# Attention and fp8 feed-forward on one core: variance from ScalarE's squares, up weights scaled in their turning product, first aggregation on GpSimd, x rounded in PSUM by TensorE, in a new order

## The chip, the cores and the metric

The kernel runs on one core of a Trainium2 chip. The metric is the device time of one execution in microseconds (us); lower is better. A time given for a kernel is the median of its runs.

## What is computed

x is 4 batches of 256 rows by 256 channels, ctx is 4 x 256 x 128. The reference, cut to what matters:

```python
# attention: energy from ctx alone, x enters normalised
query, key = ctx @ Wq.T + bq, ctx @ Wk.T + bk
attention = softmax(query @ key.T)
x = x + layernorm(x) @ attention.T
# feed-forward on layernorm(x), all three products with fp8-rounded operands
qx, sx, sc = quantize(layernorm(x))            # row scale = max|row| / 448
g = qlinear(qx, sx, sc, w_gate)                # 704 x 256 each, weight rows
u = qlinear(qx, sx, sc, w_up)                  # scaled by max|row| / 448 and rounded
t = silu(g) * u                                # 1024 x 704
qt, st, sct = quantize(t)
x = x + qlinear(qt, st, sct, w_down)           # 256 x 704
```

The rounding to fp8 is done by adding and subtracting a "grid": a number per element, a power of two times a large constant with some bits more, so that fp32's own rounding cuts the value to fp8's mantissa. `grid_w`, `grid_x`, `grid_d` and `grid_t` are these for the up and gate weights, x, the down weights and t.

## The kernel before

It is written engine by engine: every engine has a list of calls, written out by hand, that it works off in order, and semaphores join the lists. P is 128, b counts the four batches, i the eight tiles of 128 rows (two to a batch), k the six chunks of 128 gate and up rows, h halves.

**Attention.** TensorE projects q and k (`project_q`, `project_k`, one per half), forms the scores (`scores`), VectorE takes their negated maximum (`score_max`), ScalarE the exponentials (`exps`), VectorE puts 1/z on the diagonal of a 128x128 matrix (`spread_of_z`), and TensorE turns and scales the attention in one fp32 product with it (`transpose_att`, L1143). `attend` (L1154) multiplies by the rows of x, and VectorE's `residual` (L758) makes x1 out of the result, 1/std of the first normalisation and x.

**Weights.** For chunk k: VectorE takes peaks, reciprocals and scales (`peak_of_up`, `reciprocal_up`, `scales_up`), ScalarE multiplies (`scale_up`), VectorE makes the grid (`exponents_up`, `floor_up`), GpSimd adds and subtracts it (`add_grid_up`, `subtract_up`), ScalarE multiplies by the row's peak (`dequantise`, L566), TensorE turns the chunk (`transpose_up`, L1178), ScalarE copies it out of bank_a as `w_hi` (`evac_up`) and VectorE keeps the rest of the fp32 value as `w_lo` (`split_up`, L875). There is one bank for this, so `transpose_up(k)` waits for `split_up(k - 1)`, and the first `gates` waits for all six.

**x.** First statistics are of x (`bn_stats1`, `bn_aggr1`, then GpSimd's `add_eps1`, `rstd1_of`), second ones of x1 (`bn_stats2`, `bn_aggr2`). ScalarE centres x1 (`centre_x1`), VectorE takes the peak and makes the grid and the sum (`peak_of_x`, `grids_x`, `add_grid_x` L813), GpSimd subtracts (`subtract_x`, L396), TensorE turns the bf16 result (`transpose_qx`, L1166), ScalarE copies it out (`evac_qxT`).

**Feed-forward.** For each tile i, `gates(i)` and `ups(i)` (L1197) are eight matmuls each, 352 columns wide, into gate_ps and up_ps. ScalarE's `silu`, VectorE's `hidden` (t, L885), `peak_of_t`, `grids_t`, `add_grid_t`, GpSimd's `subtract_t`, TensorE's `transpose_t`, ScalarE's `evac_tT`, TensorE's `down`, VectorE's `scale_y` and a last addition follow. gate_ps and up_ps have one buffer each, so `gates(i)` waits for `silu(i - 1)` and `ups(i)` for `hidden(i - 1)`. The last tile goes in two halves.

**Down weights.** They are rounded like the others, turned by two DMA transposes on SyncE's queue, scattered to their order in device memory by six indirect DMAs that GpSimd issues (`scatter(k)`, L357), and read back; `down(0)` waits for that.

`keep_warm`, `keep_clock` (L1276) and `keep_busy` are matmuls on zeros whose results nobody reads.

## Time and profile before

| | |
|---|---|
| median of 3 runs | 80.45 us (80.34 to 80.68) |
| the profiled execution's own time | 80.45 us |
| its span, first to last instruction | 78.6 us |
| outside the span | 1.85 us |
| TensorE busy | 69.5 us, 88% |
| VectorE busy | 69.1 us, 88% |
| ScalarE busy | 52.0 us, 66% |
| GpSimd busy | 54.1 us, 69% |
| granted TensorE clock, mean of the span | 1.000 |

In the profile's rows PE is TensorE's matmuls, PEld its weight loads, DVE VectorE, ACT ScalarE, POOL GpSimd and SP SyncE; a q behind a name is that engine's sequencer. An fp32 matmul stands in two records, a transpose and a bf16 matmul in one. The ends of matmuls are modelled and overlap the next start, so that the cost of a group of them is read from its start to the start of what follows without a wait.

### The profile page before, as it was taken

To read this page: it belongs to the slowest core of one execution; us is meant where nothing else is said; L and a number is where in the kernel's file an instruction comes from. 1 tells how busy PE (TensorE), PEld (TensorE's weight loads), DVE (VectorE), ACT (ScalarE), POOL (GpSimd) and SP (SyncE) were. 2 spreads that over 40 slices of the span, in tenths; PEclk is the share of its full clock that TensorE was granted. 3 is DMA by queue.
4 is the path that set the end of the run, shared out by engine and by line. 5 is a ranking of instruction groups with operands and counts; after the bars stand their busy time and mean duration, and the time that the engine had idled before them with its cause. 6 is when DMAs were issued, how large, how long until landed. Compare 5 with 4: busy or idle time off the path is not lost.

```text
span 78.6 us, 1481 instructions
## 1 busy us (share of the span) xinstructions
PE 69.5 (88%) x449; PEld 57.7 (73%) x449; DVE 69.1 (88%) x180; ACT 52.0 (66%) x102; POOL 54.1 (69%) x66
## 2 busy tenths in 40 slices
PE   4999998999749599294999999999799999985996
PEld 4945837988549489272998999979698699744575
DVE  1019999999899999999999999999999999999860
ACT  0615799999966999897877472937924557446400
POOL 5000008973999999985687989899954667985960
DMA  0899999900000000004140201110033001030143
GB/s 18 289 389 388 330 360 397 379 20 0 0 4 4 0 0 8 0 0 91 32 77 0 75 0 33 33 38 0 17 88 112 4 22 53 0 133 0 41 159 133
DMA packets 6839, 7.33 MB, mean 93 GB/s; under 512 B 2256, under 2 KB 5200, under 8 KB 6832
## 3 DMA queue, kind: packets, MB, share of 16 engines
q1 hardware_dynamic: 6064, 5.97, 23.1%
q10 hardware_dynamic: 576, 0.92, 3.3%
q0 software_dynamic: 192, 0.36, 1.5%
q8 instruction: 3, 0.05, 0.3%
q14 instruction: 4, 0.03, 0.1%
HBM read 5.44 MB, written 1.41 MB: 87 GB/s over the span
## 4 chain that ended last, share of the span: by engine, by line
DVE 30%; POOL 25%; PE 22%; issue 15%; DMA 6%; SPq 1%; POOLq 0%; DVEq 0%
POOL q_w L407 6%; DVE t_sb L885 6%; DMA x_sb<-x_dram 6%; PE gate_ps L1197 5%; PE up_ps L1197 5%; DVE peak_w L820 4%; POOL rstd L371 3%; PE gate_ps L1269 3%; POOL sum_w L403 3%; POOL x_sb L435 3%; POOL yscale L417 2%; DVE grid_w L772 2%; PE bank_c L1154 2%; POOL q_t L424 2%; DVE peak_d L850 2%
## 5 line engine op out<-in xcount | busy, mean ns | idle before, releaser
L403 POOL TENSOR_TENSOR sum_w<-sum_w,grid_w 128x512 f32<-128x512 f32 x5 | 5.7, 1155 | 11.9 <-DVE grid_w L777 11.9
L424 POOL TENSOR_TENSOR q_t<-sum_t,grid_t 128x704 bf16<-128x704 f32 x7 | 10.9, 1554 | 3.9 <-DVE sum_t L915 3.9
L1197 PE MATMUL gate_ps<-w_hi,qxT 128*128 128x352 f32 x32 | 10.7, 337 | 1.2 <-issue 1.2
L1197 PE MATMUL up_ps<-w_hi,qxT 128*128 128x352 f32 x32 | 10.8, 340 | 0.4 <-DVE t_sb L885 0.4
L590 ACT ACTIVATE act_g<-gate_ps,rowscale 128x704 f32<-128x704 f32 x8 | 6.7, 843 | 5.3 <-PE gate_ps L1197 5.3
L1197 PE MATMUL gate_ps<-w_lo,qxT 128*128 128x352 f32 x32 | 10.3, 323 | 0.0
L1197 PE MATMUL up_ps<-w_lo,qxT 128*128 128x352 f32 x32 | 10.3, 323 | 0.0
L604 ACT ACTIVATE tT<-bank_b 128x768 bf16<-128x768 bf16 x7 | 5.7, 809 | 5.6 <-PE bank_c L1241 3.2
L1154 PE MATMUL bank_c<-attT,xT 128*128 128x256 f32 x32 | 7.7, 383 | 1.5 <-DVE x L758 1.5
L357 POOL DMA_INDIRECT wdnT_order<-wdnT,idx_sb x6 | 7.0, 1164 | 1.6 <-issue 1.6
L597 ACT ACTIVATE abs_t<-t_sb 128x704 bf16<-128x704 f32 x8 | 6.3, 786 | 2.4 <-DVE t_sb L885 2.4
L1154 PEld LDWEIGHTS bank_c<-attT,xT 128*128 128x128 f32 x32 | 5.8, 190 | 2.4 <-issue 1.7
L1197 PEld LDWEIGHTS gate_ps<-w_hi,qxT 128*128 128x128 f32 x32 | 6.0, 188 | 1.7 <-issue 1.4
L885 DVE TENSOR_TENSOR t_sb<-up_ps,act_g 128x704 f32<-128x704 f32 x8 | 7.1, 887 | 0.1
L915 DVE SCALAR_TENSOR_TENSOR sum_t<-t_sb,s_t,grid_t 128x704 f32<-128x704 f32 x7 | 6.9, 984 | 0.3
L890 DVE TENSOR_REDUCE peak_t<-t_sb 128x1 f32<-128x704 f32 x8 | 7.0, 881 | 0.0
L713 DVE BATCH_NORM_STATS2 bn<-x_sb 128x6 f32<-128x256 f32 x8 | 3.0, 413 | 4.5 <-DMA x_sb<-x_dram 4.5
L407 POOL TENSOR_TENSOR q_w<-sum_w,grid_w 128x512 bf16<-128x512 f32 x6 | 6.8, 1161 | 0.2
L1197 PEld LDWEIGHTS up_ps<-w_hi,qxT 128*128 128x128 f32 x32 | 6.0, 188 | 0.8 <-ACT qxT L547 0.7
L1197 PEld LDWEIGHTS up_ps<-w_lo,qxT 128*128 128x128 f32 x32 | 6.0, 188 | 0.0
L1197 PEld LDWEIGHTS gate_ps<-w_lo,qxT 128*128 128x128 f32 x32 | 6.0, 188 | 0.0
L566 ACT ACTIVATE sum_w<-q_w,peak_w 128x256 f32<-128x256 bf16 x12 | 5.2, 507 | 1.1 <-POOL q_w L407 1.1
(105 smaller groups left out, 190.8 us busy)
## 6 DMA issues: line engine op xcount, KB each, us to landing
x_sb<-x_dram SPq DMA_DIRECT2D x4, 256.0 KB, 8.7
xT<-x_t_dram SPq DMA_DIRECT2D x2, 512.0 KB, 8.9
out_dram<-x_sb SPq DMA_DIRECT2D x8, 128.0 KB, 1.7
wup_sb<-w_gate_up_dram ACTq DMA_DIRECT2D x3, 256.0 KB, 5.7
wup_sb<-w_gate_up_dram SPq DMA_DIRECT2D x3, 256.0 KB, 5.9
wdn_sb<-w_down_dram SPq DMA_DIRECT2D x1, 704.0 KB, 9.3
ctx_sb<-ctx_t_dram SPq DMA_DIRECT2D x2, 256.0 KB, 4.8
wdnT_in_order<-wdnT_order SPq DMA_DIRECT2D x1, 320.0 KB, 2.8
```

The costliest lines, as they stand in the source:

```text
L357: nc.gpsimd.indirect_dma_start(out=wdnT_order, out_offset=bass.IndirectOffsetOnAxis(ap=idx_sb[0:fresh[k], k:k + 1], axis=0), in_=wdnT[0:fr ...
L403: nc.gpsimd.tensor_tensor(sum_w[:, k], sum_w[:, k], grid_w[:, k], ALU.add).then_inc(sum_w_done[k], 1)
L407: nc.gpsimd.tensor_tensor(q_w[:, k], sum_w[:, k], grid_w[:, k], ALU.subtract).then_inc(q_w_done, 1)
L424: nc.gpsimd.tensor_tensor(q_t[:, i % 2], sum_t[:, i % 2], grid_t[:, i % 2], ALU.subtract)\
L590: nc.scalar.activation(halves(act_g[:, i % 3]), gate_ps[:, :, 0:IH], ACT.Silu, scale=rowscale[:, i:i + 1]).then_inc(silu_done, 1)
L597: nc.scalar.activation(abs_t[:, i % 2], t_sb[:, i % 2], ACT.Abs, scale=GRID)\
L604: nc.scalar.activation(tT[:, i % 2], tT_ps, ACT.Copy).then_inc(tT_evac, 1)
L885: nc.vector.tensor_tensor(halves(t_sb[:, i % 2]), up_ps[:, :, 0:IH], halves(act_g[:, i % 3]), ALU.mult).then_inc(t_done, 1)
L890: nc.vector.tensor_reduce(peak_t[:, i:i + 1], t_sb[:, i % 2], AX_X, ALU.max, apply_absolute_value=True).then_inc(peak_t_done, 1)
L915: nc.vector.scalar_tensor_tensor(sum_t[:, j], t_sb[:, j], s_t[:, col], grid_t[:, j], ALU.mult, ALU.add)\
L1154: last = nc.tensor.matmul(xm_ps[:, j], xT[:, b, c, j * P:(j + 1) * P], attT[:, b, c], start=(c == 0), stop=(c == NC - 1))
L1197: last = nc.tensor.matmul(ps[:, h, 0:IH], qxT[:, b, c, j * P:(j + 1) * P].bitcast(F32R), w[:, c, a, h * IH:(h + 1) * IH].bitcast(F32R), st ...
```

## The change

Five things are changed.

- The second statistics go from VectorE to others: `residual` gives the row sum as well (`accum_out`), ScalarE centres with it (everything is N times as large from there on), and ScalarE squares the centred rows and sums them (`squares_x`). `bn_stats2` and `bn_aggr2` are gone.
- `bn_aggr1` is gone; GpSimd joins the two halves of the first statistics in five small operations.
- `dequantise` is gone: the peaks stand on the diagonal of `spread_w`, made by GpSimd, and `transpose_up` is an fp32 product with it.
- `add_grid_x`, `subtract_x` and `transpose_qx` are gone: TensorE adds x times a diagonal of scales, plus the grid, minus the grid, in PSUM (`quantise_x`). GpSimd makes the diagonals (`spread_of_sx`).
- `spread_of_z` is one instruction where it was two, `yscale_of` serves two tiles at once, and all five lists and the order of the loads are new.

```diff
             def centre_x1(b):
-                act.wait_ge(stats2_done, b + 1)
+                act.wait_ge(x1_done, b + 1)
...
-                                                bias=mv2[:, i, 0:1], scale=-1.0)
+                                                bias=total2[:, i:i + 1], scale=-float(N))
                 last.then_inc(xc2_done, 1)
+            def squares_x(b):
+                act.wait_ge(xc2_done, b + 1)
+                for j in range(LT):
+                    i = LT * b + j
+                    last = nc.scalar.activation(wup_sb[:, b, j], xc2[:, b, j], ACT.Square, accum_out=var2[:, i:i + 1])
+                last.then_inc(stats2_done, 1)
...
+            def spread_of_w(k):
+                after("ident")
+                pool.wait_ge(peak_w_done, k + 1)
+                for a in range(2):
+                    last = nc.gpsimd.tensor_scalar(spread_w[:, k, a], ident[:, :], peak_w[:, k, a:a + 1], 1.0, ALU.mult,
+                                                   ALU.mult)
+                last.then_inc(spread_w_done, 1)
...
+            def spread_of_sx(b):
+                pool.wait_ge(s_x_done, b + 1)
+                after("ident")
+                for j in range(LT):
+                    i = LT * b + j
+                    last = nc.gpsimd.tensor_scalar(spread_sx[:, b, j], ident[:, :], s_x[:, i:i + 1], 1.0, ALU.mult,
+                                                   ALU.mult)
+                last.then_inc(spread_sx_done, 1)
...
                     last = nc.vector.scalar_tensor_tensor(x1[:, b, j], xm_ps[:, j], rstd1[:, i:i + 1],
-                                                          x_sb[:, b, j], ALU.mult, ALU.add)
+                                                          x_sb[:, b, j], ALU.mult, ALU.add,
+                                                          accum_out=total2[:, i:i + 1])
...
-            def transpose_qx(b):
-                pe.wait_ge(q_x_done, b + 1)
+            def quantise_x(b):
+                pe.wait_ge(xc2_done, b + 1)
+                pe.wait_ge(spread_sx_done, b + 1)
+                pe.wait_ge(grid_x_done, b + 1)
...
+                blocks = [(c, j) for c in range(NC) for j in range(LT)]
+                for c, j in blocks:
+                    nc.tensor.matmul(qxT_ps[:, c, j * P:(j + 1) * P], xc2[:, b, j, c * P:(c + 1) * P],
+                                     spread_sx[:, b, j], start=((c, j) == blocks[0]), stop=False)
+                for c, j in blocks:
+                    nc.tensor.matmul(qxT_ps[:, c, j * P:(j + 1) * P], grid_x[:, b, j, c * P:(c + 1) * P],
+                                     identb[:, :], start=False, stop=False)
+                for c, j in blocks:
+                    last = nc.tensor.matmul(qxT_ps[:, c, j * P:(j + 1) * P], grid_x[:, b, j, c * P:(c + 1) * P],
+                                            minus_identb[:, :], start=False, stop=((c, j) == blocks[-1]))
                 last.then_inc(qxT_ready, 1)
...
             def transpose_up(k):
-                pe.wait_ge(deq_done, k + 1)
+                pe.wait_ge(q_w_done, k + 1)
+                pe.wait_ge(spread_w_done, k + 1)
...
-                        last = nc.tensor.transpose(wuT_ps[:, c, a], deq_w[:, k, a, c * P:(c + 1) * P], ident[:, :])
+                        last = nc.tensor.matmul(wuT_ps[:, c, a], q_w[:, k, a, c * P:(c + 1) * P], spread_w[:, k, a],
+                                                start=True, stop=True)
```

On SyncE's queue the loads were ctx 0, x 0, up 1, up 3, ctx 1, xT 0, up 5, x 1, down, x 2, x 3, xT 1, and are now ctx 1, ctx 0, up 1, up 3, x 0, xT 0, down, x 2, x 3, up 5, x 1, xT 1.

TensorE's list from the second chunk of weights to just before the first `gates`, before; bank_a with ident is `transpose_up`, bank_c is `attend`, up_ps with spread_rz `transpose_att`, bank_b with warm_w `keep_clock` and bank_d `transpose_qx`:

```order
L1178 MATMUL bank_a<-ident,sum_w 128x128 x4
L1143 MATMUL up_ps<-spread_rz,att 128x128 x4
L1178 MATMUL bank_a<-ident,sum_w 128x128 x4
L1154 MATMUL bank_c<-attT,xT 128x256 x4
L1276 MATMUL bank_b<-warm_w 128x128 x4
L1178 MATMUL bank_a<-ident,sum_w 128x128 x4
L1143 MATMUL up_ps<-spread_rz,att 128x128 x4
L1178 MATMUL bank_a<-ident,sum_w 128x128 x4
L1166 MATMUL bank_d<-identb,q_x 128x128 x4
L1154 MATMUL bank_c<-attT,xT 128x256 x4
L1178 MATMUL bank_a<-ident,sum_w 128x128 x4
```

and the same stretch of TensorE's list now, where bank_a with spread_w is `transpose_up` and the three rows of bank_d are `quantise_x`:

```order
L1198 MATMUL bank_a<-spread_w,sum_w 128x128 x4
L1297 MATMUL bank_b<-warm_w 128x128 x6
L1154 MATMUL up_ps<-spread_rz,att 128x128 x4
L1198 MATMUL bank_a<-spread_w,sum_w 128x128 x4
L1165 MATMUL bank_c<-attT,xT 128x256 x4
L1198 MATMUL bank_a<-spread_w,sum_w 128x128 x4
L1297 MATMUL bank_b<-warm_w 128x128 x2
L1179 MATMUL bank_d<-spread_sx,xT 128x128 x4
L1182 MATMUL bank_d<-identb,grid_x 128x128 x4
L1185 MATMUL bank_d<-minus_identb,grid_x 128x128 x4
L1198 MATMUL bank_a<-spread_w,sum_w 128x128 x4
L1165 MATMUL bank_c<-attT,xT 128x256 x4
```

A rounding of x is twelve matmuls in place of four, a transpose of weights is a product, and four `keep_clock` calls of two matmuls stand in this stretch where two stood. Up to the first `gates` there are 20 matmuls of `keep_clock` now and 12 before; behind it none now and 8 before.

GpSimd's list around the scatters, before; q_x is `subtract_x`, q_t is `subtract_t`, the DMA rows are `scatter`:

```order
L396 TENSOR_TENSOR q_x<-sum_x,grid_x 128x512
L357 DMA wdnT_order<-wdnT,idx_sb 704x256 x2
L390 TENSOR_TENSOR rowscale<-rstd,peak_x 128x2
L396 TENSOR_TENSOR q_x<-sum_x,grid_x 128x512
L357 DMA wdnT_order<-wdnT,idx_sb 704x256
L424 TENSOR_TENSOR q_t<-sum_t,grid_t 128x704
L357 DMA wdnT_order<-wdnT,idx_sb 704x256 x2
L390 TENSOR_TENSOR rowscale<-rstd,peak_x 128x2
L396 TENSOR_TENSOR q_x<-sum_x,grid_x 128x512
L424 TENSOR_TENSOR q_t<-sum_t,grid_t 128x704
```

and now:

```order
L450 TENSOR_SCALAR spread_sx<-ident,s_x 128x128 x4
L358 DMA wdnT_order<-wdnT,idx_sb 704x256
L405 TENSOR_SCALAR ve<-var 128x4
L358 DMA wdnT_order<-wdnT,idx_sb 704x256 x4
L466 TENSOR_TENSOR q_t<-sum_t,grid_t 128x704
L411 TENSOR_TENSOR rstd<-ve,minus_half 128x4
L417 TENSOR_TENSOR rowscale<-rstd,peak_x 128x2 x2
L450 TENSOR_SCALAR spread_sx<-ident,s_x 128x128 x2
L466 TENSOR_TENSOR q_t<-sum_t,grid_t 128x704
```

Five scatters now stand ahead of the first `subtract_t`, and the second half's 1/std, row scales and the last `spread_of_sx` stand behind that. Further down the list, `subtract_t(4)` stands ahead of `subtract_t(3)`.

## Rows read from the trace of the kernel before

**Rows 1.** Page, part 1: busy time, share, instructions.

```profile
PE 69.5 (88%) x449; PEld 57.7 (73%) x449; DVE 69.1 (88%) x180; ACT 52.0 (66%) x102; POOL 54.1 (69%) x66
```

**Rows 2.** Page, part 4: the chain that ended last, by engine.

```profile
DVE 30%; POOL 25%; PE 22%; issue 15%; DMA 6%; SPq 1%; POOLq 0%; DVEq 0%
```

**Rows 3.** Busy time by stretch (start:end, length, engines, clock, DMA share, GB/s).

```profile
1.10:20.60 19.50, 19.13 (x90) 14.50 (x90) 14.90 (x41) 14.65 (x37) 7.37 (x10) 1.00 0.73 259
20.60:37.53 16.93, 11.74 (x77) 10.05 (x76) 16.57 (x55) 14.46 (x33) 15.14 (x15) 1.00 0.07 14
37.53:65.64 28.11, 27.56 (x192) 25.18 (x193) 27.65 (x65) 18.07 (x28) 21.90 (x25) 1.00 0.15 40
```

**Rows 4.** Timeline of TensorE, first 17 us (start, us, what, idle before).

```profile
1.11 2.93 PE L1281 MATMUL gate_ps<-warm_w 128*128 128x128 f32 x12 [1.11 <-DVE warm_w L956]
...
13.37 1.13 PE L1143 MATMUL up_ps<-spread_rz,att 128*128 128x128 f32 x8 [0.16 <-DVE spread_rz L749]
14.34 1.06 PE L1276 MATMUL bank_b<-warm_w 128*128 128x128 f32 x8
```

**Rows 5.** Timeline of TensorE, 24 to 38 us.

```profile
24.49 0.60 PE L1178 MATMUL bank_a<-ident,sum_w 128*128 128x128 f32 x4
24.93 1.06 PE L1143 MATMUL up_ps<-spread_rz,att 128*128 128x128 f32 x8
26.88 0.63 PE L1178 MATMUL bank_a<-ident,sum_w 128*128 128x128 f32 x4 [0.89 <-DVE w_lo L875]
...
29.07 1.05 PE L1276 MATMUL bank_b<-warm_w 128*128 128x128 f32 x8
29.96 0.62 PE L1178 MATMUL bank_a<-ident,sum_w 128*128 128x128 f32 x4
...
32.91 0.63 PE L1178 MATMUL bank_a<-ident,sum_w 128*128 128x128 f32 x4 [1.44 <-DVE w_lo L875]
33.68 0.40 PE L1166 MATMUL bank_d<-identb,q_x 128*128 128x128 bf16 x4
33.92 1.95 PE L1154 MATMUL bank_c<-attT,xT 128*128 128x256 f32 x8
...
37.53 0.40 PE L1197 MATMUL gate_ps<-w_hi,qxT 128*128 128x352 f32 x1 [1.23 <-issue]
```

**Rows 6.** VectorE, groups by line and shape (busy us, mean ns).

```profile
L813 DVE SCALAR_TENSOR_TENSOR sum_x<-xT,s_x,grid_x 128x256 f32<-128x256 f32 x8 | 3.5, 480 | 0.0
L758 DVE SCALAR_TENSOR_TENSOR x<-bank_c,rstd,x_sb 128x256 f32<-128x256 f32 x8 | 3.5, 474 | 0.4 <-POOL rstd L371 0.4
...
L713 DVE BATCH_NORM_STATS2 bn<-x 128x6 f32<-128x256 f32 x8 | 2.9, 408 | 0.0
...
L718 DVE BATCH_NORM_AGGREGATE mv<-bn 128x2 f32<-128x6 f32 x16 | 2.0, 164 | 0.0
```

**Rows 7.** ScalarE and GpSimd, groups by line and shape.

```profile
L566 ACT ACTIVATE sum_w<-q_w,peak_w 128x256 f32<-128x256 bf16 x12 | 5.2, 507 | 1.1 <-POOL q_w L407 1.1
...
L521 ACT ACTIVATE att<-gate_ps,neg_max 128x256 f32<-128x256 f32 x8 | 3.7, 477 | 0.1
...
L521 ACT ACTIVATION_READ_ACCUMULATOR att<-gate_ps,neg_max 128x1 f32 x8 | 1.7, 210 | 0.0
...
L424 POOL TENSOR_TENSOR q_t<-sum_t,grid_t 128x704 bf16<-128x704 f32 x7 | 10.9, 1554 | 3.9 <-DVE sum_t L915 3.9
L357 POOL DMA_INDIRECT wdnT_order<-wdnT,idx_sb x6 | 7.0, 1164 | 1.6 <-issue 1.6
...
L444 POOL CAST identb<-ident 128x128 bf16<-128x128 f32 x1 | 0.3, 291 | 0.1
```

**Rows 8.** DMA issues of SyncE's queue at 1.1 us (KB, us to landing).

```profile
x_sb<-x_dram SPq DMA_DIRECT2D x1, 256.0 KB, 4.4
```

**Rows 9.** Timeline of VectorE behind the last tile's peak.

```profile
69.11 0.87 DVE L890 TENSOR_REDUCE peak_t<-t_sb 128x1 f32<-128x704 f32 x1
...
70.46 0.53 DVE L781 TENSOR_SCALAR grid_t<-abs_t,s_t 128x384 bf16<-128x384 bf16 x2
```

More of the change, by code:

```diff
@@ L148, in build @@
         sum_w = sb("sum_w", [P, KC, 2, N])
-        q_w = sb("q_w", [P, KC, 2, N], BF16)
-        deq_w = sum_w
+        q_w = sum_w
+        spread_w = sb("spread_w", [P, KC, 2, P])
         w_hi = sb("w_hi", [P, NC, 2, I])
@@ L806, in grids_x @@
                 last.then_inc(grid_x_done, 1)
-            def add_grid_x(b):
-                dve.wait_ge(grid_x_done, b + 1)
-                for j in range(LT):
-                    i = LT * b + j
-                    last = nc.vector.scalar_tensor_tensor(sum_x[:, b, j], xc2[:, b, j], s_x[:, i:i + 1],
-                                                          grid_x[:, b, j], ALU.mult, ALU.add)
-                last.then_inc(sum_x_done[b], 1)
             def peak_of_up(k):
@@ L1007, in _ @@
-            bn_aggr2(1)
-            reciprocal_x(0)
+            split_up(0)
+            exponents_up(2)
+            reciprocal_of_z(2)
+            spread_of_z(2)
+            residual(0)
+            reciprocal_down()
+            bn_stats1(3)
+            reciprocal_of_z(3)
+            spread_of_z(3)
+            split_up(1)
+            floor_up(2)
+            peak_of_x(0)
+            add_grid_up(4)
+            reciprocal_x(0)
+            residual(1)
+            split_up(2)
+            scales_x(0)
@@ L1082, in _ @@
             scales_t(6)
+            scale_y(1)
             hidden(7)
@@ L1302, in _ @@
             attend(0)
-            transpose_up(0)
-            attend(1)
             transpose_up(1)
             transpose_att(2)
+            attend(1)
             transpose_up(2)
-            attend(2)
             keep_clock(2)
             keep_clock(2)
+            keep_clock(2)
+            transpose_att(3)
             transpose_up(3)
-            transpose_att(3)
+            attend(2)
             transpose_up(4)
-            transpose_qx(0)
+            keep_clock(2)
+            quantise_x(0)
+            transpose_up(5)
             attend(3)
-            transpose_up(5)
             gates(0)
```

348 lines of the change are left out of this document (161 added, 187 removed).

## The prediction

> **What bounds the kernel now.** I read the page from the top. The busy shares [rows 1] name no single bound: TensorE and VectorE both stand at 88%. The chain that ended last [rows 2] gives VectorE 30% of the span, GpSimd 25%, TensorE 22% and "issue", time with no cause that is seen, 15%. The stretches [rows 3] are of more use, and the reader is to compare the first and the third number of each. From 20.60 us to the first `gates` at 37.53, VectorE is busy for 16.57 of 16.93 us and TensorE for 11.74. From there to the end of the last `ups` at 65.64, VectorE has 27.65 of 28.11 us and TensorE 27.56. Before 20.60 TensorE has 19.13 of 19.50. So VectorE is full from the first weights on, and TensorE is full in two stretches of three: all its slack is 5.2 us between 20.60 and 37.53, 0.4 before it and 0.55 behind. The timeline [rows 5] says what that slack was: `transpose_up` waits 0.89 and 1.44 us for VectorE's `split_up`, and the first `gates` 1.23.
>
> **What the change takes from VectorE.** Eight `add_grid_x` take 3.5 us of busy time, eight statistics of x1 2.9, sixteen aggregations 2.0 [rows 6]. Neighbours overlap by about 0.08 us each, 32 instructions, so that this is 8.4 - 2.6 = 5.8 us of VectorE's time; joining the instructions of `spread_of_z` gives some 0.6 more. Against this stands the row sum that `residual` now writes. No instruction of VectorE in the trace does so. The bounds are nothing and the 0.48 us of one whole `add_grid_x` for each of eight, 3.8 us; I take 0.1, since ScalarE's read of its accumulator, the nearest row, is 0.21 with an overlap of about 0.1 [rows 7]. VectorE is relieved by 5.6 us: alone, that would be a large gain.
>
> The Trainium skill (VectorE: DVE Perf Modes, section Two Vector instructions with no wait between them) says that an op that also writes its accumulator is two instructions, the main one and a read. This trace shows it for ScalarE alone, as a record of 0.21 us; by the rule VectorE gets eight more short instructions, which is my 0.1 each.
>
> **What it costs TensorE.** I read costs from start to start, since the records' ends are modelled. An fp32 turn with a diagonal, `transpose_att`, takes 14.34 - 13.37 = 0.97 us [rows 4]; its other record, 1.06 us long like that of a `keep_clock` group whose distance to the next start is 29.96 - 29.07 = 0.89, allows 0.89 [rows 5]. `transpose_up` as a transpose takes 24.93 - 24.49 = 0.44 us. As a product it has the shape of `transpose_att`: + 0.45 to 0.53 us, six times, + 2.7 to 3.2. `transpose_qx` takes 33.92 - 33.68 = 0.24 for four bf16 matmuls. `quantise_x` is four fp32 products and eight such bf16 ones, 1.37 to 1.45 us: + 1.1 to 1.2 each, four times. `keep_clock` is 0.89 / 4 = 0.22 us a matmul: eight more before the first `gates` are + 1.8, eight fewer behind it - 1.8.
>
> The Trainium skill (TensorE: Matmul & The Clock Gate, section Terms) has transpose mode four times as fast for fp32. By that a product would take 4 x 0.44 = 1.8 us and the six would add 8 us. The row of `transpose_att` shows about 0.9 for the very shape, so that the ratio here is two.
>
> Up to the first `gates` that is 2.7 to 3.2, 1.1 to 1.2 and 1.8: 5.6 to 6.2 us. TensorE's idle time there is 5.2 + 0.4, and since each record before a wait seems 0.17 longer (1.06 against 0.89) than it occupies, seven waits hide 1.2 more: 6.8 us. With no wait left the first `gates` starts 0.6 to 1.2 us earlier. Behind it come three `quantise_x`, + 3.4 to 3.6, less 1.8 of `keep_clock`, less the idle 0.55 + 0.35: + 0.7 to 0.9. The last `ups` so ends between 0.5 us earlier and 0.3 later with TensorE never waiting; I take 0.1 earlier. This is a floor, and VectorE's relief cannot lower it.
>
> **Waits that come back.** Following the lists with the rows' durations I find TensorE's handoffs close in the weights' ring (`transpose_up`, `evac_up`, `split_up`) but met, because `dequantise` (12 activations of 0.51 [rows 7]) has left ScalarE and the `split_up` calls have less ahead of them. The squares put 8 x (0.48 + 0.21) back on ScalarE, less overlaps; they stand in front of the first two `silu`, and the second `gates` waits for the first `silu`: up to 0.3 us. On GpSimd five scatters in a row take 5 x (1.16 + 0.27) = 7.2 us [rows 7], from about 40.4, my estimate for the landing of the second DMA transpose; `subtract_t(0)` (1.55 us) ends near 49.1, `subtract_t(1)` near 52.7 and, behind the last scatter, `subtract_t(2)` near 56.2. TensorE comes to `transpose_t(2)` at about 55.9, so that it waits 0.3. I count 0.4 for both. The diagonals that GpSimd makes, 20 of 128x128, are not in the trace: at least a cast of that size, 0.29 us, and at most a whole 128x704 subtraction, 1.55 [rows 7]; by size (128 columns of 704) 0.28, so I take 0.3. Ten are made before the first grid is there, when GpSimd has nothing else to do; at 1.55 each they would take 15.5 us from the first peak on and everything would slip by some 8 us, the far end, to which I give no chance of its own, since a row of 0.29 is the nearest in size and kind.
>
> **What is hidden.** ctx's first half now lands where x's did, 1.2 + 4.4 = 5.6 us [rows 8]; the six warm-up matmuls took 2.93 us [rows 4], ten take 4.9, to 6.0, which covers it. The first projection is 1.0 us later than by its data, but that is four matmuls moved, not added. Up 5, x 1 and x 0 land later and are read later (VectorE's list has them behind the down peaks).
>
> **The end.** From `hidden(7)` on VectorE does the same work. Of 70.46 - 69.11 = 1.35 us from the last peak to its grids [rows 9] the peak is 0.87 and some 0.3 was latency of two tiny operations, which `scale_y(2)` now fills: - 0.3. The sum: -0.1 + 0.4 - 0.3 = 0.0, on a span of 78.6 and a profiled time of 80.45, which is the median too. I forecast **80.4 us**, with 79.8 to 81.0 for this case: -0.4 and +0.2 are the bounds of TensorE's products, the rest the waits.
>
> **Rivals.** (1) *VectorE's relief arrives.* TensorE's floor is lower than I read, because products with a diagonal hide half their length behind their neighbours, as weight loads do. For: VectorE and GpSimd lead the chain [rows 2]. Against: `transpose_att` alone took 0.97. Half the added 2.7 + 4.5 us is 3.6 of which waits eat back a third: 80.4 - 2.4 = 78.0; this case reaches from there to 79.8. Chance 0.27. (2) *Slower: the ring of weights keeps TensorE waiting.* `transpose_up(k)` waits for `split_up(k - 1)`, and behind it `attend`, `quantise_x` and `gates` all stand in TensorE's list. It cost 0.89 + 1.44 = 2.3 us before; that was covered by slack, and now each wait adds to a full list. If it costs 1.5 us again: 80.4 + 1.5 = 81.9. It decides from 0.5 us of waits. Chance 0.26. (3) *The accumulating `residual` costs double*, 0.48 us more each. Two pairs stand in front of a `split_up` that is needed at once, + 1.0: 81.4. For it speaks that the Trainium skill (Vector Engine (DVE) Microarchitecture Reference, its list of pitfalls) halves the throughput of this instruction with two SBUF sources that are not bf16; against, that `sum_x` has two such sources without an accumulator and takes the same 0.48 as `residual` with one [rows 6]. Chance 0.04. (4) *The scatters cost more*: if the first starts 2 us later, `transpose_t(0)` to `(2)` each wait, 82.5. Chance 0.03. The forecast has 0.40.
>
> **The numbers.** A difference below 0.5%, 0.4 us, cannot be told from none here: faster is below 80.05, slower above 80.85. Rival 1 is all faster; of the forecast a fifth lies below, a sixth above. Faster 0.27 + 0.08 = 0.35; slower 0.26 + 0.04 + 0.03 less a little of rival 2 inside the bound, and 0.06 of the forecast: 0.35; same 0.30. The range takes in most of rivals 1 and 2: 78.8 to 81.9.
>
> **What would show it.** In the changed kernel's profile: TensorE over 97% busy from 1.1 us to the last `ups`, with `gates` first at 36.4 to 37.2 and the last `ups` ending at 65.2 to 66.2; VectorE with 4 us of idle time between the first and the last `hidden`; rows of 0.9 to 1.0 us for the products of `transpose_up`; no reader of q_w or spread_w waiting. Waits of TensorE on w_lo over 1 us in total would mean rival 2; a `quantise_x` below 1.0 us rival 1; an extra VectorE record of more than 0.2 us behind `residual` rival 3. A granted clock below 1.00 in any stretch would break the sum, which has it at full throughout [rows 3].

## Result and the profile after

The changed kernel took 82.01 us (median; 81.72 to 82.42), the kernel before 80.41 on the same chip: ratio 1.0185, 95% interval 1.0151 to 1.0219. Forecast were 80.4 us and 78.8 to 81.9: it is slower, and lies just outside the range. I measured it twice more later, as a yardstick: 1.0109 (1.0061 to 1.0157) and 1.0111 (1.0046 to 1.0177). By the three ratios its loss is 0.9 to 1.5 us. Here and below a ratio leaves out executions over 1.5% slower than the fastest of the same kernel, and a median does not, which is why the two disagree for "phased, no clock". The profiled execution took 81.72 us with a span of 79.9: 1.3 us more span than before.

Page, part 1, of the changed kernel; then its chain by engine; then its busy time by stretch (up to the first `gates`, to the last `ups`; columns as in [rows 3]):

```profile
PE 75.2 (94%) x521; PEld 64.9 (81%) x521; DVE 66.8 (84%) x152; ACT 51.1 (64%) x106; POOL 56.9 (71%) x88
```

```profile
PE 68%; DVE 12%; DMA 8%; issue 7%; SPq 1%; ACT 1%; DVEq 0%
```

```profile
1.11:20.60 19.49, 18.84 (x103) 15.79 (x104) 13.25 (x31) 13.78 (x32) 11.23 (x24) 1.00 0.75 259
20.60:37.16 16.56, 16.35 (x116) 14.32 (x115) 15.56 (x42) 13.68 (x36) 15.86 (x22) 1.00 0.03 8
...
37.16:67.05 29.89, 28.95 (x212) 26.67 (x212) 28.25 (x57) 19.29 (x34) 21.80 (x29) 1.00 0.16 41
```

Against [rows 1 to 3]: TensorE has 5.7 us more and leads the chain. The first `gates` comes at 37.16, 0.37 earlier than in [rows 3]. The stretch from there to the last `ups` lasts 29.89 us in place of 28.11: 1.8 us are lost in this one stage. Behind it 12.85 us are left in place of 12.96. VectorE's busy time fell by 2.3 us (69.1 to 66.8), where the prediction had 5.6. That is the odd number, and the timeline of VectorE in the feed-forward stage shows why:

```profile
46.99 0.89 DVE L912 TENSOR_TENSOR t_sb<-up_ps,act_g 128x704 f32<-128x704 f32 x1
47.80 0.14 DVE L805 TENSOR_SCALAR s_t<-rec_t 128x1 f32<-128x1 f32 x1
47.92 0.89 DVE L917 TENSOR_REDUCE peak_t<-t_sb 128x1 f32<-128x704 f32 x1
48.72 2.09 DVE L818 TENSOR_SCALAR grid_x<-abs_x,s_x 128x256 bf16<-128x256 bf16 x2
...
51.29 0.95 DVE L942 SCALAR_TENSOR_TENSOR sum_t<-t_sb,s_t,grid_t 128x704 f32<-128x704 f32 x1
52.37 0.89 DVE L912 TENSOR_TENSOR t_sb<-up_ps,act_g 128x704 f32<-128x704 f32 x1
```

GpSimd at that time, and the two waits of TensorE behind it:

```profile
42.24 1.25 POOL L358 DMA_INDIRECT wdnT_order<-wdnT,idx_sb  x1 [1.83 <-DMA wdnT<-q_d]
...
48.00 0.95 POOL L358 DMA_INDIRECT wdnT_order<-wdnT,idx_sb  x1 [0.31 <-issue]
48.97 1.55 POOL L466 TENSOR_TENSOR q_t<-sum_t,grid_t 128x704 bf16<-128x704 f32 x1
```

```profile
51.29 0.43 PE L1218 MATMUL gate_ps<-w_hi,qxT 128*128 128x352 f32 x1 [0.21 <-ACT qxT L610]
53.41 0.40 PE L1218 MATMUL up_ps<-w_hi,qxT 128*128 128x352 f32 x1 [0.57 <-DVE t_sb L912]
```

The two grids of x take 2.09 us; elsewhere in the same profile such a pair takes 0.47, and in the kernel before:

```profile
48.63 0.48 DVE L781 TENSOR_SCALAR grid_x<-abs_x,s_x 128x256 bf16<-128x256 bf16 x2
```

The long pair lies beside GpSimd's subtraction (48.97 to 50.52) and ends 0.3 us behind its end. `hidden(3)`, behind them in VectorE's list, starts at 52.37, and `ups(4)` waits for it. The Trainium skill (SBUF — State Buffer, section Who interferes with whom) gives the rule: a VectorE instruction in a two-port mode excludes GpSimd and is excluded by it for a whole instruction, and one with two SBUF inputs contends with a GpSimd instruction that reads SBUF. This trace agrees: `hidden` (one input in PSUM) and `peak_of_t` (a reduction) keep their 0.87 to 0.89 us, grids of x, of t and of the down weights and a scaled sum of the down weights do not. Which mode an instruction ran in, the trace does not show. In all, seven VectorE instructions of the changed kernel are longer than their like, by 0.27, 0.33, 0.92, 0.39, 0.53, 1.62 and 0.45 us (4.5 in all), each beside a GpSimd instruction. In the kernel before there are three, by 0.23, 0.20 and 0.16.

### The profile page after: what moved, and what is told of

Read it like the earlier page. It is cut to its first block, busy times and chain, and to the rows that moved or that the text cites. A ratio compares the mean times of both kernels' runs of the same rounds, so it can differ in the third digit from the quotient of the medians.

```text
span 79.9 us, 1630 instructions
## 1 busy us (share of the span) xinstructions
PE 75.2 (94%) x521; PEld 64.9 (81%) x521; DVE 66.8 (84%) x152; ACT 51.1 (64%) x106; POOL 56.9 (71%) x88
## 4 chain that ended last, share of the span: by engine, by line
PE 68%; DVE 12%; DMA 8%; issue 7%; SPq 1%; ACT 1%; DVEq 0%
PE up_ps L1218 11%; PE bank_c L1165 9%; PE gate_ps L1218 8%; PE bank_a L1198 8%; DMA wup_sb<-w_gate_up_dram 8%; PE gate_ps L1290 5%; PE up_ps L1154 5%; PE bank_c L1262 4%; PE bank_d L1179 3%; PE bank_b L1297 3%; DVE peak_w L847 3%; PE bank_a L1262 3%; PE bank_b L1248 3%; DVE t_sb L912 2%; PE gate_ps L1138 2%
## 5 line engine op out<-in xcount | busy, mean ns | idle before, releaser
L847 DVE TENSOR_REDUCE peak_w<-wup_sb 128x2 f32<-128x512 f32 x6 | 3.9, 672 | 6.1 <-DMA wup_sb<-w_gate_up_dram 6.1
L358 POOL DMA_INDIRECT wdnT_order<-wdnT,idx_sb x6 | 6.3, 1044 | 3.2 <-DMA wdnT<-q_d 1.8
L426 POOL TENSOR_SCALAR spread_w<-ident,peak_w 128x128 f32<-128x128 f32 x12 | 4.3, 375 | 5.8 <-DVE peak_w L847 5.8
L438 POOL TENSOR_TENSOR sum_w<-sum_w,grid_w 128x512 f32<-128x512 f32 x6 | 6.9, 1157 | 0.2
L434 POOL TENSOR_TENSOR sum_w<-sum_w,grid_w 128x512 f32<-128x512 f32 x5 | 5.7, 1155 | 1.5 <-DVE grid_w L814 1.5
L1198 PE MATMUL bank_a<-spread_w,sum_w 128*128 128x128 f32 x48 | 6.6, 281 | 0.1
L1198 PEld LDWEIGHTS bank_a<-spread_w,sum_w 128*128 128x128 f32 x48 | 5.8, 191 | 1.2 <-issue 1.0
```

Source lines behind the costliest of these rows:

```text
L358: nc.gpsimd.indirect_dma_start(out=wdnT_order, out_offset=bass.IndirectOffsetOnAxis(ap=idx_sb[0:fresh[k], k:k + 1], axis=0), in_=wdnT[0:fr ...
L438: nc.gpsimd.tensor_tensor(q_w[:, k], sum_w[:, k], grid_w[:, k], ALU.subtract).then_inc(q_w_done, 1)
L847: nc.vector.tensor_reduce(peak_w[:, k], wup_sb[:, k], AX_X, ALU.max, apply_absolute_value=True).then_inc(peak_w_done, 1)
L1198: last = nc.tensor.matmul(wuT_ps[:, c, a], q_w[:, k, a, c * P:(c + 1) * P], spread_w[:, k, a], start=True, stop=True)
```

## Experiments

Landmarks from each profile (us). "Stage 1" is from the first `gates` to `hidden(4)`, "stage" from the first `gates` to `hidden(7)`, by starts. Ratios are to the kernel before on the same chip; 1.011 to 1.0185 is the yardstick. Beside a measurement of the unaltered changed kernel on the same chip stand only "phased, down later", "phased, grids left out", "apart, no clock" and "phased to the end"; for the others its ratio on their chip is not known.

| kernel | median | ratio (95%) | first gates | stage 1 | stage |
|---|---|---|---|---|---|
| before | 80.4 to 80.9 | 1 | 37.53 | 17.90 | 28.37 |
| changed | 82.01 | 1.0185 (1.015, 1.022) | 37.16 | 18.95 | 30.40 |
| changed, again | 81.81 | 1.0109 (1.006, 1.016) | 37.41 | 18.92 | 30.37 |
| changed, third | 82.13 | 1.0111 (1.005, 1.018) | 37.70 | 18.96 | 30.41 |
| scatters apart | 81.95 | 1.016 (1.008, 1.024) | 36.73 | 18.74 | 30.33 |
| turn undone | 86.89 | 1.076 (1.063, 1.089) | 41.75 | 17.74 | 29.66 |
| rounding undone | 86.55 | 1.073 (1.065, 1.081) | 38.16 | 21.78 | 33.24 |
| squares alone | 90.9 | 1.117 (1.105, 1.128) | 44.71 | 21.71 | 32.19 |
| no clock | 81.73 | 1.010 (1.007, 1.013) | 36.84 | 18.90 | 30.36 |
| more clock | 82.70 | 1.022 (1.018, 1.027) | 38.88 | 17.97 | 29.44 |
| more clock, before | 82.0 | 1.009 (1.005, 1.013) | 39.26 | 17.83 | 28.31 |
| grids apart | 81.60 | 1.011 (1.005, 1.017) | 36.77 | 18.58 | 30.57 |
| grids left out | 81.75 | 1.009 (1.005, 1.013) | 37.34 | 18.75 | 30.20 |
| squares undone | 83.67 | 1.035 (1.031, 1.040) | 39.56 | 18.36 | 30.04 |
| phased | 84.1 | 1.039 (1.034, 1.043) | 37.80 | 17.64 | 32.53 |
| phased, no clock | 84.12 | 1.017 (1.013, 1.021) | 37.85 | 17.63 | 32.51 |
| phased, down later | 82.70 | 1.021 (1.017, 1.026) | 37.50 | 17.64 | 31.15 |
| phased, grids left out | 82.34 | 1.022 (1.017, 1.027) | 36.31 | 17.42 | 30.92 |
| apart, no clock | 82.17 | 1.016 (1.011, 1.020) | 36.90 | 18.58 | 30.57 |
| phased to the end | 81.39 | 1.009 (1.005, 1.013) | 37.24 | 17.65 | 29.90 |

The stage lengths repeat within 0.05 us in three profiles of the changed kernel; the ratios of one and the same kernel moved by 0.008. So small differences are read from the landmarks.

**The parts undone.** The order is the changed kernel's, so a part's loss includes that the order was not made for it.

```diff
-            subtract_t(0)            # behind scatter(4)
+            subtract_t(0)            # GpSimd: ahead of scatter(3)
```

> The changed kernel with one call moved: the first subtract_t stands behind the third scatter and no longer behind the fifth. Theory A (a collision: GpSimd's first subtraction of t runs beside VectorE's last grids of x, which took 2.09 us where the same pair takes 0.48 elsewhere, and the fourth hidden and the fifth ups wait): the grids take 0.5 us again and the time falls by 0.8 to 1.2 us, to 81.0. Theory B (TensorE's list is simply full, the stall is hidden): no change, 82.0 within 0.3.

`hidden(3)` came at 50.50 and not 52.37 (the first `gates` 0.4 earlier), but now the grid of tile 2 met GpSimd's next subtraction, and TensorE waited 1.1 us for q_t:

```profile
52.66 1.63 DVE L818 TENSOR_SCALAR grid_t<-abs_t,s_t 128x704 bf16<-128x704 bf16 x1
```

The stage is as long as before the edit (30.33 us for 30.40), and the time is not the 81.0 of theory A. Late scatters alone are not the cause; the collision moved.

```diff
-                nc.tensor.matmul(wuT_ps[:, c, a], q_w[..], spread_w[:, k, a], ...)
+                nc.tensor.transpose(wuT_ps[:, c, a], deq_w[..], ident[:, :])   # and dequantise(k) on ScalarE
```

> The changed kernel with the weights' turn put back: ScalarE multiplies by the peaks again and TensorE transposes. TensorE has 6 x 0.45 = 2.7 us less, all before the first gates, ScalarE 4.9 us more. Theory B (TensorE full): the first gates starts 1.5 to 2.7 us earlier, 79.5 to 80.5. Rival (the ring of weights through ScalarE and VectorE sets the pace anyway): 82.0 or slower.

TensorE waited 8.4 us for ScalarE's dequantised weights, and the first `gates` came at 41.75. ScalarE has 5.2 us of dequantising more [rows 7], beside the squares that it has taken on: 4.8 us lost by the ratios (1.076 against 1.016 of "scatters apart" on the same chip). Three of its four executions had a granted clock under 1.00 in the mean; the profiled one had 1.00, and was 4.3 us longer than that of "scatters apart".

```diff
-            quantise_x(b)            # TensorE: product, grid on, grid off
+            transpose_qx(b)          # and add_grid_x on VectorE, subtract_x on GpSimd
```

> The changed kernel with the rounding of x put back on VectorE and GpSimd: TensorE has 4 x 1.1 = 4.4 us less, VectorE 3.2 us and GpSimd 4.5 us more. Theory B (TensorE full): faster by 1 to 3 us, 79 to 81, the gain limited by VectorE, which is full again. Rival (VectorE is the engine that matters and the rounding on TensorE pays): slower by 1 to 3 us, 83 to 85.

TensorE's waits, by what it waited for (us, times, longest):

```profile
PE up_ps L1220 <- DVE t_sb L918: 4.8, 2, 2.7
PE bank_a L1200 <- DVE w_lo L908: 2.1, 2, 1.2
...
PE bank_d L1187 <- POOL q_x L448: 0.8, 1, 0.8
```

Rounding on TensorE thus pays in this order: without it 4.6 us are lost by the ratios, though it costs TensorE 4 x (1.37 - 0.24) = 4.5. Some of the 4.6 is the clock's, whose mean was 0.98 in all four executions: at most 0.02 x 84.2 = 1.7 us, an estimate.

```diff
-            bn_stats2(b); bn_aggr2(b)                  # kernel before, VectorE
+            squares_x(b)                               # ScalarE, behind centre_x1(b)
```

> The kernel before with one part of the change alone, in its own order: x1's statistics by residual's row sum and ScalarE's squares. VectorE has 3.2 us less between 20 and 38 us and TensorE nothing more. Theory B (VectorE's relief pays where TensorE has slack and costs it nothing): faster by 1 to 2.5 us, 78 to 79.4. Rival (relief of VectorE is worth nothing, since GpSimd's 1/std of the second statistics comes later through ScalarE): 80.4 or slower.

This misled more than it told. GpSimd's list was the kernel before's, and its `add_eps2` waited 5.10 and 8.31 us for the squares with subtractions and scatters queued behind it; TensorE's granted clock fell to 0.943 of full in the mean. It says only that a late producer needs its consumer moved in the list too. The cleaner question, the squares undone in the changed kernel:

```diff
-            squares_x(b)                               # changed kernel, ScalarE
+            statistics2(b); aggregate2(b)              # VectorE; residual without its row sum
```

> The changed kernel with the variance of x1 made by VectorE again (eight bn_stats, eight bn_aggr, no row sum in residual, no squares on ScalarE), placed where the residuals stand in the new order; the other parts stay. VectorE gets 8 x 0.36 + 8 x 0.12 us less overlaps, about 3.3 us, of which three quarters before the first gates; ScalarE gets 4.8 us less. Theory A, VectorE is near full before the first gates (15.93 of 16.93 us there in the changed kernel), so its relief was worth something and only paid for what TensorE was given: the first gates at 38.3 to 39.5 us (37.16), ratio 1.035 to 1.055. Theory B, TensorE is the bound there, so that VectorE's relief is worth nothing: first gates at 37.0 to 37.6, ratio 1.015 to 1.022.

Some 3.3 us more on VectorE moved the first `gates` to 39.56, by 1.9 to 2.4 us against the three profiles of the changed kernel. So VectorE's relief was worth its time before the first `gates`: it paid there for a part of what TensorE was given. The ratio of 1.035 is at the lower end of what theory A had.

**The clock's matmuls.**

```diff
-            keep_clock(2)            # all ten calls ahead of gates(0)
```

> The changed kernel without the ten keep_clock calls ahead of the first gates (20 matmuls on zeros, 0.22 us each by the rows, 4.4 us of TensorE's list; nothing of the result is changed). Theory B (TensorE's list is full): the first gates starts earlier by as much as the other engines allow, at least 1 us, and the time falls below 81. Rival (the pace of that stretch is set by the weights' ring and GpSimd; TensorE only looks full): gates where it was, 82.0. Theory C (the clock needs them): a granted clock below 1.00 and 83 or more.

TensorE lost 4.4 us of work there and the first `gates` came 0.3 us earlier; the rest turned into waits, with the granted clock of the profile at 1.00:

```profile
PE bank_a L1198 <- DVE w_lo L902: 1.9, 2, 1.3
PE up_ps L1154 <- ACT att L575: 1.7, 1, 1.7
```

Three of its eleven executions had a mean clock of 0.979, and none of the changed kernel's sixteen did. The time of 81.73 is neither below 81 nor 83 or more; the rival, that other handoffs set the pace of that stretch, is the nearest.

```diff
             transpose_att(3)
+            keep_clock(4); keep_clock(4)
             transpose_up(3)
```

> The changed kernel with eight more matmuls on zeros between the fourth transpose_att and the fourth transpose_up, 1.8 us of TensorE's list. Theory B (full list, no slack): + 1.5 to 1.8, 83.6. Rival: + 0 to 0.5.

Eight matmuls (1.8 us) delayed the first `gates` by 1.7 against the first profile of the changed kernel, and by 1.5 and 1.2 against the two later ones, which share a wait of 1.1 us at `transpose_up(1)` with this run: TensorE had at most 0.6 us of slack in that stretch. Together with the run before: TensorE and the handoffs to it are close to each other, since less work for it won 0.3 us and more work cost over 1.2. At `hidden(7)` only 0.2 to 0.8 us of the delay were left. TensorE's list was later, GpSimd's nearly as before, and the collision of `grid_x(3)` was 1.10 us long instead of 2.09:

```profile
50.45 1.10 DVE L818 TENSOR_SCALAR grid_x<-abs_x,s_x 128x256 bf16<-128x256 bf16 x2
```

That made the stage 0.96 us shorter (29.44 for 30.40) with no operation of it changed. Eight such matmuls in the kernel before, at its three waits:

> The kernel before with eight more such matmuls at the three places where TensorE waited (before the third and the fifth transpose_up and before the first gates). Theory B (slack of 5.2 us takes them): 80.4, + 0 to 0.4. Rival (TensorE was the bound before as well): + 1.5 to 1.8, 82.1.

This execution's context arrived late (scores at 10.19 us in place of 8.25), so its first `gates` cannot be read; the ratio of 1.009 says that about 0.7 of 1.8 us was not covered, which lies between the two forecasts.

**Is TensorE the bound of the stage?** Here my account fell.

```diff
                 for c, j in blocks:  # quantise_x(1), (2), (3): the eight bf16 products left out
-                    nc.tensor.matmul(qxT_ps[..], grid_x[..], identb[:, :], ...)
-                    nc.tensor.matmul(qxT_ps[..], grid_x[..], minus_identb[:, :], ...)
```

> The changed kernel with the eight bf16 products that add and take off the grid left out of quantise_x(1), (2) and (3), so that x of three sequences is scaled and turned but not rounded. Everything else, orders too, stays. The eight products of one take 0.42 us from start to start in the changed kernel (0.22 + 0.20), so that TensorE has 1.26 us less between the first gates and the last ups, and no other engine has anything less. Theory A, TensorE is full in the feed-forward stage and sets its length: the last hidden starts 1.0 to 1.3 us earlier than the 67.56 us of the changed kernel, ratio to the kernel before 1.003 to 1.007 (from 1.0185). Theory B, the stage is paced by GpSimd's subtractions and VectorE's stretched instructions: TensorE's saved time comes back as waits for q_t or t_sb of over 0.8 us in all, the last hidden starts less than 0.4 us earlier, ratio 1.014 to 1.019. The grid work of VectorE is still done.

With 1.26 us less on TensorE the last `hidden` started at 67.54 (67.56 in the changed kernel), and counted from the first `gates` 0.20 us earlier. The rest came back as waits:

```profile
50.56 0.51 PE L1252 MATMUL bank_b<-identb,q_t 128*128 128x128 bf16 x6 [0.81 <-POOL q_t L466]
53.39 0.40 PE L1222 MATMUL up_ps<-w_hi,qxT 128*128 128x352 f32 x1 [0.99 <-DVE t_sb L912]
```

Theory B held by its landmark and its waits: the collision sets `hidden(3)`, and TensorE is merely busy until then. Its ratio of 1.014 to 1.019 did not come, but 1.009, which the unaltered kernel also reached later (1.011).

**Moving the collision away.** First VectorE's list alone: the last grids of x and the grids of tile 1 forward of `peak_of_t(2)`, and the sums of tiles 1 and 2 and the grids of tile 2 to other places near `hidden(3)` (not shown):

```diff
             scales_t(1)
-            peak_of_t(2)
             grids_x(3)
+            grids_t(1)
+            peak_of_t(2)
```

> The changed kernel with VectorE's list reordered between the third and the fourth hidden and just behind it: the last grids of x and the second and third grids of t stand where GpSimd runs no tensor operation. Theory A (collision): grids of 0.3 to 0.5 us each, the fourth hidden at 50.6 in place of 52.4, and 0.7 to 1.0 us less in all, 81.2. Theory B alone: 82.0, since another wait takes its place.

```profile
48.93 1.94 DVE L942 SCALAR_TENSOR_TENSOR sum_t<-t_sb,s_t,grid_t 128x704 f32<-128x704 f32 x1
```

The grids of x took 0.47 us again, but the scaled sum now stood beside the same subtraction and took 1.94 us for 0.94: an instruction with two SBUF inputs (t in fp32, its grid in bf16) is held like a grid. `hidden(3)` came at 51.15, where 50.6 was expected, and the stage was no shorter (30.57 us). I first read the ratio of 1.011 as a gain, but the unaltered kernel has the same. The next two runs are the two small edits together, "apart, no clock", and that kernel:

> The two small edits of e1 and e4 together: the ten calls of keep_clock ahead of the first gates left out, and the grids of x moved away from GpSimd's first subtraction. If both gains are real and of different stages: ratio to the changed kernel of this group 0.982 to 0.988. If they are one gain seen twice, or none: 0.992 to 1.000.

> The changed kernel itself, unaltered, as the yardstick of this group of runs. If the ratios of different chips can be compared, it is at 1.016 to 1.021 as in the first measurement (1.0185). If it comes out at 1.009 to 1.013, then the small gains read for e1 and e4 (1.0099 and 1.0108) and f1 (1.0092) were no gains of theirs.

1.016 beside 1.011 on the same chip: no gain. Then a phase: VectorE does `hidden(i)` and `peak_of_t(i)`, which do not exclude GpSimd, while GpSimd subtracts, and grids and sums between.

```diff
             hidden(3)
             peak_of_t(3)
             reciprocal_t(3)
+            grids_x(3)               # from ahead of grids_t(1)
             scales_t(3)
             grids_t(2)
@@ GpSimd
-scatter(0) add_eps2(1) scatter(1..4) subtract_t(0) rstd2_of(1) rowscale_of(2) .. subtract_t(1) scatter(5) .. subtract_t(2)
+add_eps2(1) scatter(0) rstd2_of(1) rowscale_of(2) .. scatter(1) subtract_t(0) scatter(2) subtract_t(1) scatter(3) scatter(4) subtract_t(2) scatter(5)
```

> The changed kernel with another order on VectorE and GpSimd in the feed-forward stage: VectorE does hidden(i) and peak_of_t(i) in a row, then the grids and the scaled sum of tile i - 1, and GpSimd subtracts tile i - 1 while VectorE is in the next hidden and peak; spread_of_sx(3), rstd2_of(1) and two row scales go between the first scatters, and the last three scatters go behind the subtractions of tiles 1 and 2. No operation is added or removed. Theory A, the collisions (a grid of 2.09 us in place of 0.48 and a late subtraction) cost 0.6 to 1.0 us over TensorE's floor: no VectorE instruction of the stage over 0.2 us longer than its like, TensorE waits under 0.3 us in the stage, the last hidden at 66.5 to 66.9 us (67.56 in the changed kernel), ratio 1.005 to 1.010 (from 1.0185, and 1.0108 with the grids alone moved). Theory B, the order of the two engines is not what costs, and TensorE has no time to give: ratio 1.015 to 1.019, last hidden above 67.3.

Stage 1 fell from 18.95 to 17.64 us, with the grids of x at 0.49 us, where GpSimd did not subtract. The rest of the forecast failed: the ratio was 1.039. After stage 1 `down(0)` waited for the reload of the down weights, issued at 59.25 us in place of 57.09 behind the later scatters, and TensorE's granted clock was 0.69 from 62.52 to 68.00 us, behind the wait:

```profile
62.52 0.71 PE L1262 MATMUL bank_c<-wdnT_in_order,tT 128*128 128x256 bf16 x5 [2.36 <-issue]
```

> The order of f2_phased, and the ten calls of keep_clock ahead of the first gates left out as in e1_no_clock. If the two gains are of two stages and add up (e1 had 0.009 of the time, f2 is expected to have 0.009 to 0.013): ratio 0.997 to 1.003, first gates at 36.7 to 36.9, last hidden 66.2 to 66.6. If they are the same time seen twice, since in e1 the last hidden also came earlier: ratio 1.005 to 1.010, not under that of f2 by more than 0.003. A granted clock under 0.99 would make it slower than f2.

Its profile has the same stage lengths with 7.1 us of waits, and no gain. Here the clock did fall where the matmuls on zeros are gone: behind the wait for att at 13.31 us it was 0.50 (the lower level, 1.2 GHz) from 15.0 to 17.0 us, where "no clock" with the same list up to there had kept 1.00. Two of the six executions had 1.00 throughout and took 82.2 and 82.3 us; all six of "phased" had 0.979 and took 83.5 or more. None of those two was profiled, so what the edit is worth without a dip stays open. Next the last scatter ahead of `subtract_t(2)`, and `down(0)` behind `ups(6)`:

> The order of f2_phased, with the last scatter ahead of GpSimd's subtract_t(2), down(0) one place later in TensorE's list (behind ups(6)), transpose_t(2) behind ups(5), and scale_y(0) and add_residual(0) later to match. No operation added or removed. Theory A, collisions are the loss of the stage: from the first gates to the last hidden 29.1 to 29.6 us (30.40 in the changed kernel, 32.53 in f2), down(0) waits under 0.3 us, ratio to the changed kernel of this group 0.985 to 0.993. Theory B, what the order gives in one place it takes in another (subtract_t(2) later, the reload again): 30.2 us or more, ratio to the changed kernel 0.997 or more.

Stage 1 was 17.64 again, but `ups(6)` waited 1.5 us for `hidden(5)` (VectorE had two grids and two sums in a row ahead of it), and ScalarE's `evac_tT(2)`, which waits for `down(0)`, held up `absolute_t(5)` behind it. The stage of 31.15 us and a ratio of 1.021 beside 1.011 are what theory B had. With the grid products left out of it:

> g1 with the eight bf16 products of quantise_x(1), (2) and (3) left out as in f1, so that x of three sequences is not rounded: TensorE has 1.26 us less in the feed-forward stage. If TensorE is the bound once the collisions are gone, the last hidden comes 0.9 to 1.3 us earlier than in g1. If VectorE and GpSimd pace the stage also then, less than 0.4 us and TensorE waits for t_sb or q_t by what it saved.

Stage 1 became 0.22 us shorter for 0.84 us less of TensorE (two of the three groups lie in it), and the whole stage 0.23: less than 0.4, so that by the forecast VectorE and GpSimd pace it also then. TensorE has no idle time in stage 1 of the phased order, but the others stand only 0.2 us behind it. Last, the phase to the end of the stage: VectorE's tile 4 behind `peak_of_t(5)`, GpSimd's tile 3 before 4, `absolute_t(5)` ahead of `evac_tT(2)`.

> The changed kernel, unaltered, as the yardstick. First gates to last hidden 30.4 us (30.40 and 30.37 in its two profiles); ratio to the kernel before 1.010 to 1.019.

> g1_phased_down_later with the phase kept to the end of the stage: VectorE does grids and sum of tile 4 behind hidden(5) and peak_of_t(5) and not ahead of them, GpSimd subtracts tile 3 before tile 4, and ScalarE does absolute_t(5) ahead of evac_tT(2). No operation added or removed. Theory A, the loss was one of order: from the first gates to the last hidden 29.0 to 29.6 us (30.40 in the changed kernel, 31.15 in g1), TensorE waits under 0.4 us in the stage, ratio to the changed kernel of this group 0.985 to 0.992. Theory B, VectorE has too much for it in any order, so that what is spared before hidden(4) is lost behind it: 30.2 us or more, ratio to the changed kernel over 0.996.

Busy time by stretch, first `gates` to `hidden(4)` to the last `ups` (h1_phased_to_the_end):

```profile
37.24:54.89 17.65, 17.65 (x136) 17.25 (x137) 16.37 (x40) 12.77 (x25) 13.89 (x20) 1.00 0.14 33
54.89:66.20 11.31, 10.92 (x80) 9.42 (x77) 10.76 (x17) 6.53 (x9) 7.08 (x8) 1.00 0.17 45
```

The grids of x, which took 2.09 us, take 0.48 here, beside a scatter (52.54 to 53.52) and no subtraction:

```profile
52.82 0.48 DVE L818 TENSOR_SCALAR grid_x<-abs_x,s_x 128x256 bf16<-128x256 bf16 x2
```

TensorE is not idle for 17.65 us and then for 0.39; the stage up to the last `ups` is 28.96 us, 0.93 less than in the changed kernel. Its last `hidden` starts at 67.14, behind `scale_y(1)`, so that part of the gain was not passed on. Two grids still meet GpSimd (0.94 and 0.88 us for 0.39). Ratio 1.0086 against 1.0111 of the yardstick on the same chip: 0.9975, and 0.990 to 1.005 with both intervals taken together, not to be told from none. Theory A's 29.0 to 29.6 us to the last `hidden` were missed at 29.90, and so was its ratio. What it says of the cause holds up to the last `ups`; for the whole time a gain is not shown, and no version beat the kernel before.

## Why the prediction failed

**What TensorE was given: right.** `quantise_x(3)` takes 56.48 - 55.11 = 1.37 us, forecast 1.37 to 1.45:

```profile
55.11 1.11 PE L1179 MATMUL bank_d<-spread_sx,xT 128*128 128x128 f32 x8
56.06 0.39 PE L1182 MATMUL bank_d<-identb,grid_x 128*128 128x128 bf16 x4
56.28 0.39 PE L1185 MATMUL bank_d<-minus_identb,grid_x 128*128 128x128 bf16 x4
56.48 0.41 PE L1218 MATMUL gate_ps<-w_hi,qxT 128*128 128x352 f32 x1
```

`transpose_up` is 29.54 - 28.58 = 0.96 us, forecast 0.89 to 0.97; the Trainium skill's factor of four for fp32 (TensorE: Matmul & The Clock Gate, section Terms) would have had 1.8. The floor holds too, by the busy time of the stretches. Before the first `gates` TensorE was still idle for 0.65 + 0.21 = 0.86 us (19.49 - 18.84 and 16.56 - 16.35), 0.59 of it in one wait of `transpose_att` for spread_rz; without that it would have come 0.37 + 0.86 = 1.2 earlier, forecast 0.6 to 1.2. In the stage it was busy for 28.95 us, 0.84 more than the whole stage was in [rows 3]; forecast 0.7 to 0.9. Together -0.4 for the last `ups` with no idle time, where I took -0.1 from -0.5 to +0.3.

**The accumulating residual: right.** The Trainium skill's second instruction is there (VectorE: DVE Perf Modes, section Two Vector instructions with no wait between them), 0.08 us long and inside the next one:

```profile
22.33 0.48 DVE L794 SCALAR_TENSOR_TENSOR x<-bank_c,rstd,x_sb 128x256 f32<-128x256 f32 x1
22.73 0.08 DVE L794 DVE_READ_ACCUMULATOR x<-bank_c,rstd,x_sb 128x1 f32 x1
22.73 0.48 DVE L794 SCALAR_TENSOR_TENSOR x<-bank_c,rstd,x_sb 128x256 f32<-128x256 f32 x1
```

The pair starts 0.40 us apart with it. The 0.1 us forecast is nothing; rival 3, which doubled the time of `residual`, is false. The prediction misread the row that it set against rival 3: of the two SBUF sources of `sum_x` the grid is bf16, and `residual` has one SBUF source, so that no run here tests the halving for two sources that are not bf16.

**The diagonals: a little dear.** 0.375 and 0.388 us each, forecast 0.3:

```profile
L426 POOL TENSOR_SCALAR spread_w<-ident,peak_w 128x128 f32<-128x128 f32 x12 | 4.3, 375 | 5.8 <-DVE peak_w L847 5.8
...
L450 POOL TENSOR_SCALAR spread_sx<-ident,s_x 128x128 f32<-128x128 f32 x8 | 3.0, 388 | 0.2
```

**"Waits that come back": the step that failed.** I counted 0.4 us (up to 0.3 for the first `silu` and 0.3 for `transpose_t(2)`) and none before the first `gates`; TensorE's idle time was 0.86 before the first `gates` and 29.89 - 28.95 = 0.94 in the stage, 1.8 in all. Two things in it were wrong. The scatters began at 42.24 and not at 40.4: the second `q_d` ended at 38.50 us where it was 37.85 before, and the rest is my estimate of the landing, which was too early (the kernel before's first scatter began at 41.55). So `subtract_t(0)` ran at 48.97 and not at 47.6. Above all I took every VectorE duration from rows where GpSimd stood elsewhere, and asked of a moved list only what it waits for, not what it runs beside. So "VectorE is relieved by 5.6 us" was wrong in effect: its busy time fell by 2.3, and instructions that stood still have 3.9 us more than before (4.5 less 0.6), which is about the difference. The sum with what was measured: floor -0.4 (forecast -0.1), waits 1.8 (0.4), end -0.1 (-0.3), together +1.3 us of span (0.0), which is what the two profiles differ by. The phased order shows that the 0.94 in the stage was mostly the collisions': 0.39 were left. The other 0.84 us by which the stage grew are TensorE's added work, as forecast. Of the 0.86 ahead of the first `gates` the cause is not shown; without the clock's matmuls they came only 0.3 earlier.

Two of the signs that the prediction named came out: TensorE was busy for 64.14 of the 65.94 us to the last `ups` (97.3%), and the first `gates` came at 37.16. Two did not: the last `ups` ended at 67.05, where 65.2 to 66.2 was expected, and VectorE was idle for 1.5 us between the first and the last `hidden`, where 4 were.

**Rivals.** The time fell where rival 2 had put it (81.9), and that is luck: it got there by another mechanism. The ring's wait for w_lo is absent from the first profile of the changed kernel; in the two later ones it was 1.1 us once, at `transpose_up(1)`, over the 1 us that was rival 2's sign, but the first `gates` came only 0.25 and 0.54 us later than in the first. Behind that wait too stood a collision, here a scale of four columns (0.16 us else) beside one of GpSimd's 128x512 operations (profile of the changed kernel, again):

```profile
15.75 1.11 DVE L805 TENSOR_SCALAR s_w<-rec_w 128x4 f32<-128x4 f32 x1
```

Of the twenty profiles seven have this scale at 1.0 us or more. In six of these `transpose_up(1)` waited 1.1 us for w_lo; in the seventh the clock had fallen ahead of it. In the thirteen others it did not wait for w_lo.

Rival 1, products that hide half their length, is false: `transpose_up` takes 0.96 us and `quantise_x` 1.37. Undoing the squares, the turn or the rounding in the changed kernel's order cost 1.4 to 2, 4.8 and 4.6 us, so that each part is worth its time in that order; together with the new order they do not pay for TensorE's added work. How much each would be worth in an order made for it is not known. Rival 4 has the right place (the first scatter 1.8 us late, GpSimd's subtraction behind them 1.4) and the wrong consequence: not `transpose_t` waited but VectorE.

**What stays open.** The collisions are shown to set the stage's length up to the last `ups`; that the whole time would fall by as much without them is not shown. Whether an order without any collision in all stages would beat the kernel before was not found: the best came to 1.0086. The new order was also never tried with the kernel before's operations alone. Why the ratio of the same kernel is 1.0185 once and 1.011 twice is not known; the ring's wait does not explain it, since it stands in the two lower ones.

## What to carry to other kernels

Before counting work taken off a full engine as time, look at what the engine it shares ports with does in the same microseconds: a list that is moved by a microsecond can turn a pair of instructions of 0.47 us into 2.09. An engine that is 97% busy is not thereby the bound; take work off it and see whether the landmark moves. And measure the unaltered kernel again beside each small variant: two small edits here seemed to gain 0.8% (1.010 and 1.011 where the changed kernel had 1.0185) until the unaltered kernel measured 1.011 too.
